# Values and logits in one product beside the shared expert, split on GpSimd and read back; two half buffers of queries; the first group's rows later

## What is computed

```python
xn = _layernorm(x, axis=-1)
q = einsum('bte,de->btd', xn, Wq) + bq      # k, v alike
p = softmax(einsum('bqd,bkd->bqk', q, k) / 16)
z = einsum('bqk,bkd->bqd', p, v)
gates = softmax(xt @ Wg.T)                  # xt: 4096 tokens, 16 experts
scores, inds = top_k(gates, 2); scores /= sum(scores)
h = silu(einsum('td,ehd->teh', xt, We_gate)) * einsum('td,ehd->teh', xt, We_up)
y = sum over the 2 chosen experts of scores * (h @ We_down)
shared = (silu(xt @ Ws_gate.T) * (xt @ Ws_up.T)) @ Ws_down.T
y = y + sigmoid(xt @ Wsg.T) * shared
return x + z + y
```

## Time and profile before

| | us |
|---|---|
| median of 3 runs | 512.1 (512.05 to 512.42) |
| the profiled execution | 511.44 |
| its span | 509.6 |
| PE busy | 502.7 (99%) |
| DVE busy | 402.9 (79%) |
| ACT busy | 279.5 (55%) |
| POOL busy | 199.4 (39%) |

### The profile page before, as it was taken

The page is one execution under the profiler, slowest core; times in us unless marked ns, Lnnn a source line. Parts: engine busy times, 40 slices in busy tenths (PEclk is TensorE's granted clock), DMA queues, the critical chain, the costliest instruction groups (busy, mean ns, idle before and its releaser), DMA issues.

```text
span 509.6 us, 9935 instructions
## 1 busy us (share of the span) xinstructions
PE 502.7 (99%) x3411; PEld 461.4 (91%) x3411; DVE 402.9 (79%) x847; ACT 279.5 (55%) x466; POOL 199.4 (39%) x178
## 2 busy tenths in 40 slices
PE   8999999999999999999999999999999999999997
PEld 6898988888989999999999888989989898989896
DVE  5989457899997687777776389897969797888996
ACT  4787784246655464555555547463727354544651
POOL 0001021111005777777770461454453435362640
PEclk9999999999999999999999999999999999999999
DMA  8937176111113565786676730631253213120311
GB/s 305 412 124 279 81 288 243 44 52 35 60 63 114 176 197 183 237 291 194 197 141 151 264 110 29 211 98 57 84 191 101 71 62 84 49 82 28 101 45 64
DMA packets 31184, 71.27 MB, mean 140 GB/s; under 512 B 5312, under 2 KB 9792, under 8 KB 30112
## 3 DMA queue, kind: packets, MB, share of 16 engines
q1 hardware_dynamic: 23840, 51.80, 28.3%
q0 software_dynamic: 6864, 18.75, 14.3%
q10 hardware_dynamic: 432, 0.09, 0.1%
HBM read 43.34 MB, written 27.28 MB: 139 GB/s over the span
## 4 chain that ended last, share of the span: by engine, by line
PE 88%; DVE 7%; issue 2%; ACT 1%; DMA 1%; DVEq 0%
PE ps L807 55%; PE ps L1017 11%; PE ps L947 7%; PE ps L813 6%; PE ps L1049 6%; PE ps L902 1%; PE ps L964 1%; DVE acc L1430 1%; PE ps L911 1%; DVE place_hot L1522 1%; DMA acc<-in_x 1%; DVE sil L1411 1%; DVE hT L1333 1%; DVE probs_f L1674 1%; DVE pT L1333 0%
## 5 line engine op out<-in xcount | busy, mean ns | idle before, releaser
L794 POOL DMA_INDIRECT rows_y<-ytab,slot x64 | 80.8, 1262 | 84.0 <-DVE acc L1689 64.2
L764 POOL DMA_INDIRECT blk_x<-rows,row x79 | 86.1, 1089 | 47.1 <-issue 23.2
L807 PEld LDWEIGHTS ps<-vv,pT 128*128 128x128 f32 x768 | 94.6, 189 | 2.7 <-DVE pT L1333 1.7
L807 PE MATMUL ps<-vv,pT 128*128 128x258 f32 x768 | 95.8, 283 | 1.3 <-DVE pT L1333 1.3
L807 PE MATMUL ps<-xT,shared_w 128*128 128x512 f32 x384 | 92.7, 394 | 0.4 <-DVE sil L1411 0.2
L807 PEld LDWEIGHTS ps<-xT,shared_w 128*128 128x128 f32 x384 | 70.7, 188 | 15.6 <-issue 0.8
L807 PE MATMUL ps<-qT,xbT_hi 128*128 128x512 f32 x256 | 79.1, 390 | 0.0
L1017 PE MATMUL ps<-expert_w,blk_xT 128*128 x474 | 66.0, 288 | 0.4 <-DVE blk_xT L1333 0.4
L1017 PEld LDWEIGHTS ps<-expert_w,blk_xT 128*128 128x128 f32 x474 | 58.9, 190 | 0.6 <-issue 0.6
L1321 ACT ACTIVATE probs_f<-probs_f 128x1024 f32<-128x1024 f32 x32 | 33.8, 1056 | 41.9 <-DVE probs_f L1674 41.9
L1127 ACT ACTIVATE scored_t<-ps 128x1024 f32<-128x1024 f32 (+1 forms) x33 | 32.3, 995 | 43.6 <-PE ps L807 39.5
(11 more groups left out here) (167 smaller groups left out, 857.4 us busy)
## 6 DMA issues: line engine op xcount, KB each, us to landing
ytab<-blk_y SPq DMA_DIRECT2D x40, 256.0 KB, 2.9
keys<-xT SPq DMA_DIRECT2D x8, 1024.0 KB, 6.2
stage_e<-in_experts SPq DMA_DIRECT2D x16, 384.0 KB, 3.1
rows<-xn SPq DMA_DIRECT2D x8, 512.0 KB, 3.4
xbT_hi<-keys SPq DMA_DIRECT2D x8, 512.0 KB, 5.9
xbT_lo<-keys SPq DMA_DIRECT2D x8, 512.0 KB, 6.7
out<-acc SPq DMA_DIRECT2D x32, 128.0 KB, 1.7
acc<-in_x SPq DMA_DIRECT2D x7, 512.0 KB, 9.8
```

The source lines that it names most:

```text
L764: e.indirect_dma_start(out=blk_x[:, q, n, :], out_offset=None, in_=rows, in_offset=bass.IndirectOffsetOnAxis(ap=row[:, 2 * b + n:2 * b + n ...
L794: e.indirect_dma_start(out=rows_y[:, r, k, :], out_offset=None, in_=ytab, in_offset=bass.IndirectOffsetOnAxis(ap=slot[:, k, i:i + 1], axis=0),
L807: ins = e.matmul(dst, stationary(p, k), moving(q, k), start=(n == 0), stop=(n == total - 1))
```

## The change

**Values beside the shared expert.** w_v and the router's 18 columns are put next to each other into one operand `value_w` of 274 columns (`value_split`: high part on ACT, low on DVE). A new step `vals(c, n)`, one for each of the 32 tiles, multiplies xT's tile as the stationary operand with `value_w`, 6 matmuls of 274 columns into one turn bank. Its ACT part copies the 18 logits straight to where they are wanted and the 256 values to `vals_f` (a ring of 3 tiles). POOL casts the high part and subtracts for the low part into `vals_out` (ring of 3), and SP stores both to a DRAM tensor `vals` in pieces of 1 KB. The steps stand in pairs in units 3 to 21 of stage 1; `logits`, `logits_turn` and DVE's addition go. The stores of xT get steps of their own (`keys_store`).

**Values read back.** `vals_load(b)` loads high and low parts, 2 MB a batch, into `vv`; the attention's `values` steps, their copies and remainders, and the split of w_v go. Batches 0 and 1 are loaded at the start of the attention, behind `shift_in(0)` and `keys_load(1)` on SP, batches 2 and 3 in groups 3 and 5.

**Queries in two half buffers.** qT is now two tiles of 512 queries, one a group. Heads(0,0) and heads(0,1) are projected beside the last blocks, heads(1,0) in group 0, and the heads of group g+2 in group g.

**Group 0.** `rows(0)` and `rows(1)` move from between the score maxima to behind heads(1,0), ahead of `spread`. The last scores pair of group 0 is copied in two halves (`HALVED`).

The core of the diff:

```diff
-        0: ([("router_split",), ("root", 1), ("stats", 2)], [("weights_hi", 3), ("invert", 1)], []),
-        1: ([("norm", 1), ("weights_lo", 3)], [("logits", 0)], []),
+        0: ([("root", 1), ("stats", 2)], [("weights_hi", 3), ("invert", 1)], []),
+        1: ([("norm", 1), ("weights_lo", 3)], [("value_split",)], [("keys_store", 0)]),
...
-        13: ([], [("tokens_in", 4)], [("norm", 5), ("expert_split", 1)]),
+        13: ([], [*vals(3, 2, 3), ("tokens_in", 4)], [("norm", 5), ("expert_split", 1)]),
...
+                elif kind == "vals":   # PE
+                    if n == 0:
+                        e.wait_ge(xT_lo, KD * (c + 1))
+                    product(ps[:, turn_bank(("vals", c, n)), 0:VRC], lambda p, k: xT_of(c)[:, p, k, n * P:(n + 1) * P],
+                            lambda q, k: value_w[:, q, k, :], valued)
...
+                elif prev[0] == "vals":   # turn_bank
+                    e.wait_ge(vals_copied, nth[prev])
...
+                elif kind == "vals":   # ACT
+                    e.wait_ge(valued, t + 1)
+                    copied(logits_sb[:, t, :], ps[:, bank, D:VRC], logits_copied)
+                    if t >= VR:
+                        e.wait_ge(vals_lo, t - VR + 1)
+                    copied(vals_f[:, t % VR, :], ps[:, bank, 0:D], vals_copied)
...
+                elif kind == "vals":   # POOL
+                    e.wait_ge(vals_copied, t + 1)
+                    if t >= VR:
+                        e.wait_ge(vals_stored[r], 16 * (t // VR))
+                    e.tensor_copy(vals_out[:, r, HI, :], vals_f[:, r, :]).then_inc(vals_hi, 1)
+                    e.wait_ge(vals_hi, t + 1)
+                    e.tensor_tensor(vals_out[:, r, LO, :], vals_f[:, r, :], vals_out[:, r, HI, :].bitcast(F32),
+                                    ALU.subtract).then_inc(vals_lo, 1)
...
+                elif kind == "vals_load":   # SP
+                    if b == 0:
+                        e.wait_ge(blk_downed, USED)
...
+                    elif b >= 2:
+                        e.wait_ge(weighed, BT * (b - 1))
+                    for part in (HI, LO):
+                        e.dma_start(vv[:, r, part, :, 0:D].bitcast(F32), vals[b, :, part, :, :]).then_inc(vals_loaded[r], 16)
...
-        if b == PAIRS:
-            steps.append(("heads", 0, 0))
+        if b in (PAIRS - 1, PAIRS):
+            steps.append(("heads", 0, b - PAIRS + 1))
...
-    ahead = {1: split("heads", 1, 1), 2: split("heads", 2, 0), 3: split("heads", 2, 1), 4: split("heads", 3, 0),
-             5: split("heads", 3, 1), 6: split("values", 3, 1)}
-    behind = {2: split("values", 1, 1), 3: split("values", 2, 0), 4: split("values", 2, 1), 5: split("values", 3, 0)}
+    ahead = {g: split("heads", *divmod(g + 2, 2)) for g in range(1, GROUPS - 2)}
...
-    steps += [("keys_load", 1), ("shift_in", 0), ("shift_in", 1), ("heads_second", 0, 0), ("heads_split", 0, 0), ("ones",), *split("values", 0, 0)]
+    steps += [("shift_in", 0), ("keys_load", 1), ("vals_load", 0), ("shift_in", 1), ("vals_load", 1),
+              ("heads_split", 0, 1), ("ones",)]
...
-            steps += [*split("heads", 0, 1), ("heads", 1, 0), ("tops", g), ("heads_split", 1, 0),
-                      ("values", 0, 1), *spread(g), ("values", 1, 0), ("less", new),
-                      ("values_split", 0, 1), ("less", new + 1), *spread_second(g), ("probs", new), ("values_split", 1, 0),
...
+            steps += [("tops", g), *split("heads", 1, 0), *rows(new), *rows(new + 1), *spread(g), ("less", new), ("probs", new), ("less", new + 1),
+                      *spread_second(g), ("probs_hi", new), ("probs", new + 1), ("probs_lo", new), ("less", new + 2),
```

300 lines of the change are left out of this document (132 added, 168 removed).

## The result

The changed kernel takes 518.37 us (median of 4 runs, 516.74 to 518.5) beside 512.23 for the kernel before, a ratio of 1.0122 with a 95% interval of 1.011 to 1.0134. It is 1.2% slower. I had forecast 511.1 with a range of 507.5 to 515.0, and "slower" with a chance of 0.30.

The account below looks back on a forecast made before the run. PE was taken as the bound, busy 502.7 of 509.6 us. Attention -17.3, shared stage +14.3, banks +1.4 and GpSimd +0.5 made -1.1: 511.44 becomes 510.4, 511.1 beside the median; range 507.5 to 515.

Parts of the forecast that it names:

- The value tiles' price: Shared stage, PE: 6 matmuls of 274 columns cost 0.765 us a tile, 24.5 for 32 tiles.
- the shared stage's plain sum: Shared stage, PE: 24.5 us of value tiles less 6.7 of logits products and 3.5 of transposes, +14.3.
- groups 2 to 5: Attention: each loses a values step of 2.88 us with no new PE gaps, 11.5 in all (9 to 11.5).
- rival C: Slower: group 0's first weigh waits for the read-back values, price 3.8 us, 514.9 in all; chance 0.10.
- the port lock: Shared stage: VectorE two-input and GpSimd steps exclude each other; around 3 us spread over DVE, nothing for PE.
- three signs of being wrong: Shared-stage PE idle above 4 us; group 0's softmax not deciding the first weigh; gaps in groups 2 to 5.
- the configuration's term: Shared stage: GpSimd's configuration splits tile 0 about 6.5 us late, ScalarE's copy follows late; +0.5 us (0 to 1.5).
- The banks' term: Shared stage: transposes of chunks 4 to 7 wait for turn banks that value products just filled; +1.4 us (0 to 3).
- Rival D: Slower: the value tiles' split path holds up the shared stage, +3 to +4 us, 514.5 in all; chance 0.23.
- They are there at T + 11.5: Group 0: batch 1's keys land 11.5 us after heads(0,1) ends (T), a wait of 0.6.
- my chain: Group 0: maxima, all-reduce, rows, softmax steps put the first weigh at T (end of heads(0,1)) + 22.7, a 3.0 us wait.
- my 1.6 of 2.88: Group 6: removing values(3,1), 2.88 us, gains only 1.6 (0.4 to 2.9) because a scores copy waits for DVE.

Follow-up runs that it names:

- e1: Changed kernel plus an early one-column GpSimd subtraction, so that its configuration runs while GpSimd has nothing to do: 516.04 us, ratio 1.0076 to the kernel before.
- e6: Changed kernel with the copy and remainder of heads(0,0) ahead of the last hidden block: 516.22 us, ratio 1.0091; repeat 516.24 us, 1.0097.
- e2: Changed kernel with batch 0's values read back only once the keys of batch 1 have landed: 519.38 us, ratio 1.0144 to the kernel before.
- e8: e5 with group 0's first two row additions right behind the maxima and heads(1,0)'s remainder behind the first subtraction: 512.45 us, ratio 1.0014.
- e5: Changed kernel with GpSimd configured early and three transposes moved, which left PE's order unchanged: 515.57 us, ratio 1.0072 to the kernel before.
- after_again: The changed kernel run a second time, unedited: 519.07 us, ratio 1.0139 to the kernel before.
- e3: Changed kernel with group 0's softmax ahead of heads(1,0)'s remainder and its four row additions at the end: 516.18 us, ratio 1.0083.
- e11: Early configuration, early heads(0,0) split and new group 0 order together, plus group 6's first two row steps behind its fourth subtraction: 514.65 us, ratio 1.0059.

## Why the prediction was wrong

**Right.** The value tiles' price (0.77 us a tile for 0.765), on which the shared stage's plain sum (+14.3) rests; that groups 2 to 5 give all their 2.88 each (PE has no gap between the first weigh and 483 us; behind heads(1,1) 12.6 came for 13.1); the place of the configuration and of tile 0; that heads and the softmax chain bind the first weigh, not the values: in no profile did PE wait for the load of vv, so rival C was wrong. Of the port lock little came, and mostly to GpSimd: the remainder of hT took 684 ns in the median of 32 after and 686 before, 1.21 us at most in both, while GpSimd's subtraction of a tile took 741 ns in the median and up to 1.18 us. None of my three signs of being wrong came either: PE's idle time in the shared stage stayed under 4 us, the softmax decided the first weigh, groups 2 to 5 have no gaps. The time lay outside the range all the same: in stage 1 rows that stretch don't count as idle, and for group 0 the sign asked what decides the first weigh, not when.

**Wrong, the configuration's term.** I gave it 0.5 us, with an upper end of 1.5, by asking only when ScalarE's copy would arrive at the first PE product that needs it. e1 shows 2.5. This is the step that failed in stage 1. What I left out is the rest of ScalarE's queue: behind the one late copy (33.92) stood the split of the down weights, two table loads of 1.28 us, a sil and a hidden part, then VectorE's steps, and this backlog met the value tiles at 39 us and the transposes at 51 us once more (waits of 0.45 and 0.73; with the configuration early the first is gone and the second is 0.23). The banks' term (1.4) came out near: e1 stands 16.75 above before, so 2.45 above the 14.3. Three rows of transposes of 1.10 in place of 0.79, and other stretched rows, fit this, but no run isolates them. Rival D named the right stage, but its stores did little harm: SP's stores held GpSimd up for 3.4 us in all, and ScalarE waited for GpSimd once only, the 4.06 us of the configuration.

**Wrong, the keys' arrival.** This is the step that failed in group 0. "They are there at T + 11.5" took SP's delay from the kernel before (2 us) and the median landing (7.4). It was +14.3: issued from 3.2 on, since I priced the order of blk_y on VectorE's queue nowhere, and the last piece landed after 9.46. e6 moves one step and has it at +11.7 and +12.3. Why the landing takes 9.46 and not 7.4 is open; e2 shows only that it isn't the read-back.

**Wrong, what stands behind the keys.** With the keys at +11.5 my chain gave the first weigh at +22.7, and e6 has it at +23.2 with the keys at +11.7. But I let the weigh's chain start from the maxima and the all-reduce, and treated the late keys as a cost of 0.6. In the changed order the remainder of heads(1,0) and the rows stand on VectorE ahead of the subtraction that the softmax needs, so every microsecond of the keys passes to the softmax. A wait of 3.2 came and the weigh's wait stayed at 3.0. e8 takes that order away and gains 3.1 us against e5.

**Not in the forecast: the clock.** About 1.1 of the 1.6 us that the first profile's first weigh took too long, 2.3 in after_again, where it fell behind the keys, 1.9 in e6's first profile and nothing in its second.

The miss of 8.2 us (from -1.1 to +7.1) is then: 2.7 of configuration and 1.1 of other waits in stage 1, 3.0 of late keys passed on to the softmax, 0.2 ahead of the first scores, 0.7 between the start of the first weigh and heads(1,1) (1.6 of longer weigh less 0.9 of waits for copies that I had counted and that didn't come), and 0.5 in the last groups, where among others the wait for ScalarE's copy in group 7 was 1.50 and not the 1.3 that my 1.6 of 2.88 left. The 2.7 are the 3.2 of the first profile less my 0.5; from profile to profile they go down to 2.

## What to carry to other kernels

When a step is put into an engine's queue, price every step behind it on that queue, not only its first waiter; a cost that is late once is paid again wherever the backlog meets the bound engine. Where a chain starts from a load, look at what stands ahead of the load's issue, down to the copy whose store precedes it, and put nothing that depends on the load in front of work that doesn't. Work that nothing waits for is best put into a wait that exists anyway, and in small pieces: in e3 and e11 four steps in a run met the ring of their own buffers. And three costs found one by one need not add up when they are taken away together: a new order moves the next wait to another step.

## What the runs showed of the hardware

- GpSimd's first two-operand operation waited 7.66 us in the middle of the program (6.98 in after_again), and 10.89 us in e1, where it fell beside the input loads (DMA share 1.03 from 7 to 18 us); the cast just ahead of it didn't wait for this. The first library operation has a wait of its own, 6.54 before and 6.5 after. The Trainium skill ("GPSIMD Engine Reference", section 2.1, Instruction dispatch) says that the first call to freshly loaded code pays about 6 us with no instruction in the profile that shows it. The traces agree in kind, and are longer.
- The granted clock after a wait of 3 us differed between executions of the same kernel: a mean of 0.58 in one window of e6 and 1.00 in its repeat. A window of 0.50, as in after_again, lies wholly at the lower of the two levels (1.2 GHz), and the means of 0.58 and 0.73 are partly at it.
- The read-back in 1 KB pieces was not slow: while it ran beside gathers, the windows of the kernel after show 359 GB/s from 325 to 330 us.
- VectorE's two-operand steps and GpSimd's can stretch each other: one remainder of hT took 1.21 us beside a subtraction on GpSimd in place of 0.69, and the subtraction of a value tile on GpSimd that ran beside the remainder of hT at 56.9 us in the kernel after took 1.18 us in place of 0.74.
